# Threshold search of a routed expert layer: one search over 32 experts becomes four searches over groups of eight, three of them spread beside the first list and the experts

## The reference, cut to what matters

```python
cap = int(CAP_FACTOR * T / E)                      # 140
probs = jax.nn.softmax(h @ r2_w.T, -1)
topp, topi = jax.lax.top_k(probs, TOPK)
routed = (topi[..., None] == eids).any(1)
score = jnp.where(routed, probs, -jnp.inf)
idx = jnp.argsort(-score, axis=0)[:cap].T          # the tokens of each expert
...
xe = xf[idx]
up = jnp.einsum('eci,eji->ecj', xe, w_up)
gate, upv = jnp.split(up, 2, axis=-1)
ye = jnp.einsum('ecj,eoj->eco', jax.nn.silu(gate) * upv, w_down)
out = jnp.zeros((T, C)).at[idx.reshape(-1)].add((w[..., None] * ye).reshape(-1, C))
```

## Time and profile before

| | us |
|---|---|
| median of 3 runs | 755.66 |
| lowest, highest | 754.02, 760.1 |
| the profiled execution, its own time | 759.58 |
| its span | 757.7 |
| mean granted clock of TensorE | 0.93 |

### The profile page before, as it was taken

The page is one execution under the profiler, slowest core; times in us unless marked ns, Lnnn a source line. Parts: engine busy times, 40 slices in busy tenths (PEclk is TensorE's granted clock), DMA queues, the critical chain, the costliest instruction groups (busy, mean ns, idle before and its releaser), DMA issues.

```text
span 757.7 us, 17528 instructions
## 1 busy us (share of the span) xinstructions
PE 650.4 (86%) x5275; PEld 513.0 (68%) x5275; DVE 526.0 (69%) x1548; ACT 405.2 (53%) x1569; POOL 323.7 (43%) x340
## 2 busy tenths in 40 slices
PE   8788988989889898899988112899999999999992
PEld 4455655656656566566654101599999999999992
DVE  6765786867778677785988889677778645445441
ACT  2377787887878878788683555022222222222220
POOL 3443462544526435262112000435665665665643
PEclk9999999999999999999798555699999999999997
DMA  5610020200202002010101601169888988888821
GB/s 183 219 37 26 26 74 2 74 27 25 73 0 73 26 25 73 0 49 1 50 2 50 243 0 25 35 200 259 255 250 257 268 260 264 266 236 264 274 44 15
DMA packets 57852, 85.83 MB, mean 113 GB/s; under 512 B 11452, under 2 KB 28468, under 8 KB 57652
## 3 DMA queue, kind: packets, MB, share of 16 engines
q1 hardware_dynamic: 47588, 74.37, 29.7%
q0 software_dynamic: 9216, 9.76, 7.9%
q10 hardware_dynamic: 976, 0.89, 0.4%
HBM read 72.30 MB, written 12.69 MB: 112 GB/s over the span
## 4 chain that ended last, share of the span: by engine, by line
PE 51%; ACT 20%; DVE 17%; issue 7%; DMA 2%; POOL 1%; ACTq 1%; DVEq 1%; POOLq 0%
PE pair L1014 19%; ACT arena L1320 10%; PE bank L1024 10%; DVE arena L1493 4%; PE pair L1655 3%; PE pair L1646 3%; PE bank L1609 2%; ACT arena L583 2%; PE pair L515 2%; PE bank L1036 2%; ACT arena L1269 2%; PE bank L1597 1%; PE pair L1641 1%; PE bank L1003 1%; DVE we L1474 1%
## 5 line engine op out<-in xcount | busy, mean ns | idle before, releaser
L1320 ACT ACTIVATE arena<-pair,arena 112x112 f32<-112x112 f32 x512 | 174.5, 362 | 28.2 <-DVE arena L1493 19.5
L1014 PE MATMUL pair<-arena,we 128*128 128x140 f32 x1024 | 138.0, 283 | 0.7 <-ACT arena L927 0.6
L905 POOL DMA_INDIRECT rows_out<-arena,slot_row x64 | 94.4, 1475 | 95.8 <-DVE arena L958 82.6
L1014 PEld LDWEIGHTS pair<-arena,we 128*128 128x128 f32 x1024 | 128.5, 190 | 1.2 <-issue 1.2
L935 ACT ACTIVATE arena<-pair 128x140 f32<-128x140 f32 x160 | 45.9, 287 | 149.6 <-PE pair L1014 149.6
L970 DVE SCALAR_TENSOR_TENSOR arena<-arena,pair 128x140 f32<-128x140 f32 x160 | 47.5, 297 | 98.4 <-ACT arena L935 97.5
L1320 ACT ACTIVATION_READ_ACCUMULATOR arena<-pair,arena 112x1 f32 x512 | 108.6, 212 | 0.0
L894 POOL DMA_INDIRECT arena<-rows,slot_row x64 | 63.3, 989 | 85.5 <-issue 85.5
L1655 PE MATMUL pair<-tab,arena 112*112 112x112 f32 x512 | 70.2, 274 | 16.7 <-ACT arena L1320 16.6
L1024 PE MATMUL bank<-arena,we 128*128 128x140 f32 x512 | 83.7, 286 | 0.0
L1655 PEld LDWEIGHTS pair<-tab,arena 112*112 112x112 f32 x512 | 50.5, 137 | 41.4 <-ACT arena L1320 25.1
(11 more groups left out here) (214 smaller groups left out, 1196.2 us busy)
## 6 DMA issues: line engine op xcount, KB each, us to landing
we<-w_experts_in SPq DMA_DIRECT2D x192, 256.0 KB, 4.2
wa<-w_adapters_in SPq DMA_DIRECT2D x16, 384.0 KB
arena<-ctx_in SPq DMA_DIRECT2D x8, 448.0 KB, 4.5
arena<-x_in SPq DMA_DIRECT2D x8, 448.0 KB, 3.8
rows_out<-arena SPq DMA_DIRECT2D x8, 448.0 KB, 3.3
rows<-arena SPq DMA_DIRECT2D x8, 448.0 KB, 3.4
arena<-ways_in SPq DMA_DIRECT2D x1, 1024.0 KB, 5.0
arena<-rows,slot_row POOLq DMA_INDIRECT x64, 3.8
```

The costliest lines, as they stand in the source:

```text
L905: nc.gpsimd.indirect_dma_start(d["out"], bass.IndirectOffsetOnAxis(ap=slot_row[:, h, e:e + 1], axis=0), yr[e % 2][:, h, :], None, compute_ ...
L1014: last = nc.tensor.matmul(banks[m % 4][:, part * CAP:(part + 1) * CAP], w[:, col0:col0 + 128], xet[j % 2][:, c, :], start=(c == 0), stop=( ...
L1320: last = nc.scalar.activation(pr[s % 2][:, j, :], banks[BS[s % 4]][0:T, j * T:(j + 1) * T], ACT.Exp, bias=nmx[s // 2 % 2][:, s % 2, j:j + ...
```

## The change

The 32 experts are searched as four groups of eight. The scores lie with 16 chunks x 8 experts on the partitions and 224 columns for each group (`COLS`), so a count is over 224 columns, and list and search use the same layout: the laying out anew, the spreading of bounds and `half` go. Group 0's 15 rounds stand ahead of everything, with two counts on VectorE and one on ScalarE. All three counts of the other groups are made on ScalarE (`count_scalar`). Six rounds of group 1 (`AHEAD`) stand beside the list of group 0; its seventh is counted there too. Its other rounds and all of groups 2 and 3 stand beside the experts: `rounds_of` gives the unit n of each round, every second unit. In unit n TensorE makes the total (`totals`) right behind the up-projection, VectorE the narrowing behind the gating, and ScalarE the counts for it behind the tanh of unit n - 1. The steps of a list take ten units at any k, five of them with three finds, and the unrolled part of the loop is 24 experts long instead of 16.

```diff
-GROUP_OF = (4, 4, 8, 16)
-LAST_ROUNDS = {11: (0,), 12: (1,), 13: (2, 3)}
-RANKS, FOUND_AHEAD = 4, 5
...
+GROUP = 8
+LISTS = NE // GROUP
+FIRST_OF = [g * GROUP for g in range(LISTS + 1)]
+LCH = 128 // GROUP
+PER = NB // LCH
+LT = PER * T
+COLS = [slice(g * LT, (g + 1) * LT) for g in range(LISTS)]
+RANKS = 4
 LIST_PARTS = RANKS + FINDS + 1
...
-LIST_STEPS = {
-    1: [(e, k) for e in (0, 1) for k in (2, 2, 3, 3, 4, 4, 4)],
-    2: [(1, 4), (2, 4), (2, 4), (3, 2), (3, 3)] + [(3, 4)] * 4 + [(e, k) for e in (4, 5) for k in (2, 3, 3, 4, 4, 4, 4)],
-    3: [(6, 4), (7, 4), (8, 4), (8, 4)] + [(e, k) for e in range(9, 13) for k in (2, 3, 4, 4, 4)]}
-BASES_IN, PLACED_IN = {2: 2, 7: 3}, {2: 1, 6: 2, 14: 3}
-LISTED = 16
...
+AHEAD = 6
+SEARCH_FROM = (None, None, 24, 64)
+LIST_FROM = (None, 19, 57, 97)
+LIST_STEPS = [(0,), (1,), (2,), (3, 4)] + [tuple(RANKS + 1 + 3 * i + n for n in range(3)) for i in range(5)] + [(20, 21, 22)]
+assert LIST_STEPS[-1][-1] == LIST_PARTS - 1
+SLOTS_AT = len(LIST_STEPS)
+LISTED = 24
+
+
+def rounds_of(g):
+
+    at = SEARCH_FROM[g] + 2 if g > 1 else 1
+    found = {}
+    for m in range(AHEAD if g == 1 else 0, DIGITS * ROUNDS):
+        found[at] = m
+        at += 3 if m % ROUNDS == ROUNDS - 1 else 2
+    return found
...
-TAKEN = 320
-KEPT = CHB * T - TAKEN
...
-        for k in range(DIGITS):
-            for r in range(ROUNDS):
-                act.wait_ge(s_cand, (ROUNDS + 1) * k + r + 1)
-                signal(act, nc.scalar.activation(scalar_cand, ahead(r, 0, 2),
-                                                 ACT.Identity, bias=bound_at(r)), s_sc, ROUNDS * k + r + 1)
-                with nc.allow_low_precision(reason=WHOLE):
-                    nc.scalar.activation(junk[2], live[k], ACT.Sign, bias=scalar_cand[:, 0:1], accum_out=cnt[:, 2:3])
-                    nc.scalar.activation(over[:, KEPT:], live[k][:, KEPT:], ACT.Sign, bias=scalar_cand[:, 1:2],
-                                         accum_out=cnt[:, 3:4]).then_inc(s_cnt, 1)
...
+        keep_scores(act, 0, slice(0, LT), banks[2][:, 0:LT])
+        for m in range(DIGITS * ROUNDS):
+            count_scalar(act, 0, m)
+            if m == 0:
+                keep_scores(act, 1, slice(LT, 3 * LT), banks[3][:, 0:2 * LT])
+            elif m == 1:
+                keep_scores(act, 2, COLS[3], banks[2][:, LT:2 * LT])
+        for m in range(AHEAD + 1):
+            count_scalar(act, 1, m)
...
+        return 2 * (m + 1) if g == 0 else DIGITS * ROUNDS * (g + 1) + m + 1
+
+    def count_scalar(act, g, m):
+
+        k, r = divmod(m, ROUNDS)
+        mine = 1 if g == 0 else CANDS
+        act.wait_ge(s_cand, candidates(g, m))
+        signal(act, nc.scalar.activation(scalar_cand[:, 0:mine], ahead(r, 0, mine), ACT.Identity, bias=bound_at(r)),
+               s_sc, DIGITS * ROUNDS * g + m + 1)
+        with nc.allow_low_precision(reason=WHOLE):
+            for j in range(mine):
+                last = nc.scalar.activation(scalar_junk[j], live[k][:, COLS[g]], ACT.Sign, bias=scalar_cand[:, j:j + 1],
+                                            accum_out=cnt[:, CANDS - 1 - j:CANDS - j])
+        last.then_inc(s_cnt, 1)
...
-            pe.wait_ge(s_cnt, 2 * r + 2)
-            nc.tensor.matmul(banks[4][:, 0:CANDS], same, cnt[:, 0:CANDS], start=False, stop=False)
-            nc.tensor.matmul(banks[4][:, 1:2], half, cnt[:, 3:4], start=False, stop=True).then_inc(s_tot, 1)
...
+        for m in (0, 1):
+            totals(pe, 1, m, banks[7][:, 0:CANDS + 1])
+        pe.wait_ge(s_found, 1)
+        place_rows(0, 0, banks[5][0:HC, 0:GROUP])
+        for m in (2, 3):
+            totals(pe, 1, m, banks[7][:, 0:CANDS + 1])
+        pe.wait_ge(s_wake, 1)
+        keep_warm(3, ident[0:T, 0:T], tab[0:T, 0:NT])
+        pe.wait_ge(s_found, 2)
+        place_rows(0, 1, banks[6][0:HC, 0:GROUP])
+        totals(pe, 1, 4, banks[7][:, 0:CANDS + 1])
+
+    def totals(pe, g, m, out):
+
+
+        if m or g:
+            pe.wait_ge(s_cand, candidates(g, m))
+        nc.tensor.matmul(out, same, needed[:, min(g, 1), :], start=True, stop=False)
+        pe.wait_ge(s_cnt, counted(g, m))
+        nc.tensor.matmul(out[:, 0:CANDS], same, cnt[:, 0:CANDS], start=False, stop=True).then_inc(s_tot, 1)
...
+        for m in range(DIGITS * ROUNDS):
+            k, r = divmod(m, ROUNDS)
+            if r == 0:
+                begin_digit(dve, link, 0, k)
+            for j in range(2):
+                with nc.allow_low_precision(reason=WHOLE):
+                    last = nc.vector.scalar_tensor_tensor(junk[j], live[k][:, COLS[0]], bound_at(r),
+                                                          ahead(r, 3 + j, 1).to_broadcast([128, LT]), ALU.add, ALU.is_ge,
+                                                          accum_out=cnt[:, j:j + 1])
+            last.then_inc(s_cnt, 1)
+            if m == 4:
+                dve.wait_ge(s_kept, 2)
+            beside(m)
+            narrow(dve, link, 0, m, banks[4][:, 0:CANDS + 1])
...
+        bounds(link, 0)
+        list_part(dve, link, 0, 0)
+        begin_digit(dve, link, 1, 0)
         for part in range(1, RANKS):
-            list_part(dve, link, 0, part, None, banks[4][:, 16:18])
+            list_part(dve, link, 0, part, banks[4][:, 16:18])
+        narrow(dve, link, 1, 0, ending)
...
+            if i in (5, 13):
+                link(last)
+                narrow(dve, link, 1, 1 if i == 5 else 3, ending)
...
+        narrow(dve, link, 1, 4, ending)
+        begin_digit(dve, link, 1, 1)
+        dve.wait_ge(s_kept, 3)
+        for part in range(2):
+            take_digit(link, 1, 2, part)
+        for n in range(4):
+            take_digit(link, 2, n // 2, n % 2)
+        narrow(dve, link, 1, 5, ending)
+        for part in range(2):
+            take_digit(link, 2, 2, part)
+        for n in range(6):
+            take_digit(link, 3, n // 2, n % 2)
...
+    def begin_digit(dve, link, g, k):
+
+        if k:
+            link(nc.vector.tensor_scalar(over, live[k - 1][:, COLS[g]], found[:, k - 1:k], 1.0, ALU.subtract, ALU.min))
+            link(nc.vector.tensor_scalar(over, over, -1.0, ABOVE, ALU.max, ALU.mult))
+            link(nc.vector.tensor_tensor(live[k][:, COLS[g]], over, digit[k][:, COLS[g]], ALU.add))
+        link(nc.vector.memset(bound_at(0), -1.0))
+        dve.sem_inc(s_cand, 1)
+
+    def narrow(dve, link, g, m, sums):
+
+        k, r = divmod(m, ROUNDS)
+        dve.wait_ge(s_tot, DIGITS * ROUNDS * g + m + 1)
+        signal(dve, nc.vector.scalar_tensor_tensor(reached, sums, 0.0, srt[:, r * (CANDS + 1):(r + 1) * (CANDS + 1)],
+                                                   ALU.is_ge, ALU.mult, accum_out=bound_at(r + 1)),
+               s_cand, candidates(g, m) + 1)
...
+                for g in range(1, LISTS) if listing else ():
+                    at = rounds_of(g).get(n + 1)
+                    if at is not None and (g > 1 or at > AHEAD):
+                        count_scalar(act, g, at)
...
+        def search_beside(g, n):
+
+            if n == SEARCH_FROM[g]:
+                begin_digit(dve, link, g, 0)
+            at = n - LIST_FROM[g]
+            if 0 <= at < SLOTS_AT:
+                for part in LIST_STEPS[at]:
+                    list_part(dve, link, g, part, banks[6][:, 64:66])
+            elif at == SLOTS_AT:
+                list_slots(dve, g, 0, banks[6][0:HC, 0:GROUP])
+                list_slots(dve, g, 1, banks[6][0:HC, GROUP:2 * GROUP]).then_inc(s_slot, 1)
+            m = rounds_of(g).get(n)
+            if m is not None:
+                narrow(dve, link, g, m, banks[6][:, 128:128 + CANDS + 1])
+                if m == DIGITS * ROUNDS - 1:
+                    bounds(link, g)
+                elif m % ROUNDS == ROUNDS - 1:
+                    begin_digit(dve, link, g, m // ROUNDS + 1)
...
+            elif at == SLOTS_AT:
                 pe.wait_ge(s_found, 2 + g)
+                beside = [m for t, m in rounds_of(g + 1).items() if t < n] if g + 1 < LISTS else []
+                if beside:
+                    pe.wait_ge(s_cand, candidates(g + 1, beside[-1]) + 1)
...
+            m = rounds_of(g).get(n)
+            if m is not None:
+                if g > 1 and n >= LIST_FROM[g - 1] + SLOTS_AT:
+                    pe.wait_ge(s_slot, 1 + g)
+                totals(pe, g, m, banks[6][:, 128:128 + CANDS + 1])
...
-        list_bases(pe, 1, banks[7][:, 0:2])
+        totals(pe, 1, AHEAD - 1, banks[7][:, 0:CANDS + 1])
```

324 lines of the change are left out of this document (115 added, 209 removed).

## The result

The changed kernel takes **809.33 us** (median of 4 runs, 801.4 to 817.92) against 755.35 for the kernel before in the same comparison (median of 4, 754.02 to 760.1): 1.064 times as long, 95% interval 1.059 to 1.070. The forecast was 795 us in a range of 768 to 815. The profiled execution took 806.27 us (span 803.5) against 759.58 (757.7), so +46.7 us (span +45.8) where the prediction's sum said +39.1.

The account below looks back on a forecast made before the run. The prediction took TensorE to bound the experts and ScalarE's chain the search. Its terms, -19.2 + 7.8 + 41.5 + 9 = +39.1 us, on the median of 755.66 gave 794.8, forecast as 795 us, range 768 to 815.

Parts of the forecast that it names:

- Part 1: Search rounds ahead of the experts: counts over 224 columns shorten a round from 2.60 to 1.45 us, gain 19.2 us.
- Part 2: From last narrowing to first up-projection: longer list and warming matmuls that wait for group 1's rounds, loss 7.8 us.
- Part 3: Rounds inside the experts: TensorE waits behind up-projections for ScalarE's counts, 39 rounds, loss 41.5 us.
- Part 4: Lists inside the experts: VectorE's three finds a unit make gating late for TensorE, loss 9 us, 0 to 14.
- (a): Rounds inside the experts: counts are covered, a round costs only its two matmuls, kernel not slower, 753 us; chance 0.10.
- (b): Experts: the clock falls, a third of the 20 experts with rounds run at the low level, 834 us; chance 0.06.
- (c): Experts: VectorE's narrowing is late and ScalarE waits, +0.3 us a round, lists at their upper bound, 812 us; chance 0.12.
- (d): ScalarE's counts inside the experts: back-to-back passes overlap, with lists half hidden, 780 us; chance 0.12.

Follow-up runs that it names:

- best try: Changed kernel with at most three finds a unit, totals later, counts shared with VectorE, row copy first, five rounds ahead, later searches: 770.81 us, ratio 1.019.
- Slots later: Changed kernel with two empty units between a list's last finds and the placing of its rows and slots: 802.86 us, 1.061 times the kernel before.
- thin lists: Changed kernel with finds spread over more units (four at k = 4, one or two elsewhere) and placing two units behind the last: 787.68 us, ratio 1.033.
- last try: Best try with lists dealt by VectorE's room in each unit and rounds beside lists counted by ScalarE alone: 766.52 us, 1.012 times the kernel before.

## Why the prediction came out as it did

**Part 1, rounds ahead: right.** 17.5 + 1.15 us were forecast from the start of the search to its last narrowing and 18.7 measured. The search also began 1.9 us sooner, of which I had counted 0.5; starts of the search vary by more than that from run to run.

**Part 2, to the first expert: right in kind, 1.3 us too dear.** 26.2 us where I had said 27.5. The order is the one described: warming ends, the slots are placed at 463.7, then TensorE waits for round 5 (its total at 467.19), and the last warming matmuls follow. Each came 0.7 to 1.4 us sooner behind the last narrowing than I had it.

**Part 3, rounds inside the experts: right.** 41.5 us for 39 rounds, 1.06 each; measured 36.98/35 = 1.06 each, with the chain at 2.06 instead of 2.12 us. The agreement of the sum is better than its parts: the small matmuls, put at 0.22, cost about 0.12 where nothing waits (best try), and the rest lies in the waits and in what they delay.

**Part 4, the lists: the term that was mis-sized.** I said 9 us and at most 14. Parts 1 and 2 together came out 2.7 us better than forecast and hid a little of it, and the total stayed 6 us inside the range. Of the expert stage's 59.9 us, 39 rounds at 1.06 are 41.3; the rest is 18.5 (less than the 21.4 above, since the experts of the kernel before took some more than 7.95 us too). I had compared the volume of VectorE's work with the room in its units, and by that alone a list costs 3.6 us, all of it as late gating. The late gating is there, and at 4.8 us for the three lists it is less than I had. Left out was what else stands in the queue behind the finds: the placing, for which TensorE stops (6.7 us in the three lists, by the waits at L641); the narrowing, behind which ScalarE's three counts start late; and the low clock, about 5 us where TensorE was busy at it (the sum of 2 us times one less the clock over the low windows of the second and third list). Slots later and thin lists show the first two. The clock fell behind the waits for gating twice and behind a stop at the placing once. In last try, where TensorE's longest wait from 470 to 720 us is 1.6 us, it stays at 1.00; in thin lists it does so at the lists and falls behind a wait of 2.43 us away from them. Each fall looked at thus stands behind a stop of TensorE, and one of them needed no list. Thin lists moved both the finds and the placing, so the 17.2 us it saved are not split between the two; that slots later alone gave 1.5 us in the expert stage speaks for the finds. These shares overlap and are not exact.

**The rivals.** (a) fell: the counts are not covered, and the price is the wait. When it is nearly taken away (best try, 0.12 us a round in the first experts) the lists still cost too much, so its point, 0.29 us a round for rounds and lists together, was not reached by any version. (b) held in small: not a third of 20 experts, but some 4 us at a time, three times in all. The Trainium skill (TensorE: Matmul & The Clock Gate, HAM oscillation — how this bites in real kernels) describes a kernel whose repeated waits for transfers, some 3 to 5 us each, throttle the clock each time. The trace agrees that short waits need not do it: the clock is 1.00 through all the waits of 0.7 to 1.2 us in every second unit (34.23 of 40 us busy). But it also fell behind waits of 0.78 and 1.11 us at the finds, far shorter than the page's. (c) was right about the mechanism, beside the lists only: the narrowing does come late there and ScalarE does wait for it. That the 809 measured lies near its 812 is luck in part: most of its surcharge was 0.3 us on every round, and the rounds cost what I had said. (d) fell: the passes follow each other 0.48 and 0.47 us apart and last 0.48 and 0.47. The overlap that the Trainium skill (ScalarE: Activation LUTs, What ACT_TABLE_LOAD costs) gives as about 93 ns is in the rows, but between tanh and candidates (475.99 + 0.29 against 476.17) and between a pass and the reading of its sum (the reading starts at 476.88, the pass ends at 476.97, and the next starts with that). The second was in my durations already. The first was not: the first pass starts 0.50 us behind the start of the tanh, where I had 0.60; with 0.04 us more for the three passes that is the difference between 2.12 and 2.06.
